# GpSimd's gather loops in two edge stages: the copy of the next indices ahead of the wait for landed gathers, and two rounds in one turn of the loop

## The reference

```python
# third layer (convolution): y = node features after a small matmul
x0e, x1e = y0[edge_src], y1[edge_src]                  # gather by source
m = products of w(edge_scalars), x0e/x1e and edge_sh    # message of an edge
sums = segment_sum(m, edge_dst)                         # sum by destination
# fourth layer (attention)
k = (node_feats @ wk)[senders]; v = (node_feats @ wv)[senders]   # gather by source
alpha = (q[receivers] * w_ij * k).sum(-1) / 4 * cutoffs
out = segment_sum(alpha[..., None] * v, receivers) / 16
```

## Time and profile before

| | us | share of the span |
|---|---|---|
| profiled execution, device time | 9110.68 | |
| its span | 9108.8 | |
| TensorE busy | 7570.4 | 83% |
| VectorE busy | 6053.3 | 66% |
| ScalarE busy | 5236.3 | 57% |
| GpSimd busy | 3425.6 | 38% |
| convolution stage, first to last gather | 3550.8 to 6092.7 | 28% |
| attention stage, first to last gather | 6198.7 to 9056.2 | 31% |

### The profile page before, as it was taken

One profiled execution on the slowest core, in us unless ns is written; L12 is line 12 of the kernel. 1 busy time (PEld: TensorE's weight loads), 2 busy tenths in 40 slices (PEclk: granted clock), 3 DMA queues, 4 the chain that ended last, 5 costly groups with the idle time before them and its releaser, 6 DMA issues. The chain is left out here.

```text
span 9108.8 us, 195691 instructions
## 1 busy us (share of the span) xinstructions
PE 7570.4 (83%) x51013; PEld 5736.6 (63%) x51014; DVE 6053.3 (66%) x12579; ACT 5236.3 (57%) x9302; POOL 3425.6 (38%) x4082
## 2 busy tenths in 40 slices
PE   5999999888869998989998877887777777777775
PEld 3655666577769996666666555555565556555654
DVE  7888998899964446555555555556566656666656
ACT  3666666688757775444444433345556656666653
POOL 0000000000000002666666666655555556566655
PEclk8999999999989998999999888778889888898886
DMA  3333333466646661222222211114555555555554
GB/s 113 138 135 135 137 138 136 153 225 225 213 141 183 183 183 60 63 63 63 63 63 63 55 45 45 45 43 151 159 161 166 161 156 165 166 162 162 165 160 128
DMA packets 511184, 1177.41 MB, mean 129 GB/s; under 512 B 98171, under 2 KB 171308, under 8 KB 491685
## 3 DMA queue, kind: packets, MB, share of 16 engines
q1 hardware_dynamic: 381834, 858.67, 28.9%
q0 software_dynamic: 129280, 317.93, 12.5%
HBM read 899.64 MB, written 276.57 MB: 129 GB/s over the span
## 5 line engine op out<-in xcount | busy, mean ns | idle before, releaser
L2271 POOL DMA_INDIRECT att_kv_rows<-kv_dram,att_stage x1616 | 1632.7, 1010 | 629.7 <-issue 439.2
L2011 POOL DMA_INDIRECT conv_rows<-y_dram,conv_stage x1616 | 1563.3, 967 | 642.2 <-issue 557.3
L695 PE MATMUL conv_part<-conv_msgs,conv_hot 128*128 128x256 f32 x3232 | 939.7, 443 | 0.0
L842 PE MATMUL att_mlp<-mlp_feats,mlp_w 64*128 64x512 f32 x1568 | 522.5, 742 | 435.6 <-ACT mlp_hid L862 429.0
L2034 PEld LDWEIGHTS conv_w_ps<-conv_w,conv_hid 100*128 100x128 f32 x3248 | 466.0, 221 | 656.8 <-issue 314.2
L1967 ACT ACTIVATE conv_hid<-conv_hid_ps 100x512 f32<-100x512 f32 x408 | 243.5, 597 | 1093.7 <-PE conv_hid_ps L2029 701.5
L2086 DVE TENSOR_TENSOR conv_t<-conv_rows,conv_harm 128x384 f32<-128x384 f32 x404 | 226.1, 560 | 953.8 <-DMA conv_rows<-y_dram,conv_stage 947.2
L2034 PE MATMUL conv_w_ps<-conv_w,conv_hid 100*128 100x128 f32 x3248 | 553.6, 322 | 308.1 <-DVE conv_msgs L2100 228.1
L851 PE MATMUL att_mlp<-mlp_w,mlp_hid 128*128 128x128 f32 x6272 | 790.8, 288 | 19.2 <-issue 18.8
L851 PEld LDWEIGHTS att_mlp<-mlp_w,mlp_hid 128*128 128x128 f32 x6272 | 773.1, 204 | 35.7 <-issue 35.2
L695 PEld LDWEIGHTS conv_part<-conv_msgs,conv_hot 128*128 128x128 f32 x3232 | 701.4, 228 | 105.2
(11 more groups left out here) (278 smaller groups left out, 15928.7 us busy)
## 6 DMA issues: line engine op xcount, KB each, us to landing
c_dram<-count_counts SPq DMA_DIRECT2D x392, 392.0 KB, 2.4
mean_counts<-c_dram SPq DMA_DIRECT2D x343, 448.0 KB, 3.4
w_dram<-mlp_w SPq DMA_DIRECT2D x404, 256.0 KB
att_w_rows<-w_dram SPq DMA_DIRECT2D x404, 256.0 KB
soft_counts<-c_dram SPq DMA_DIRECT2D x98, 1024.0 KB, 4.9
mlp_feats<-in_feats SPq DMA_DIRECT2D x405, 192.0 KB
soft_counts<-c_dram SPq DMA_DIRECT2D x49, 1088.0 KB, 5.0
att_lanes<-lo_dram SPq DMA_DIRECT2D x404, 128.0 KB
```

What stands on the lines that cost most here:

```text
L695: ins = nc.tensor.matmul(part, c.hot[:, s, t, :], rows[:, t, :], start=half == 0 and t == 0, stop=half == 1 and t == T - 1)
L842: nc.tensor.matmul(self.hid_ps[:, n], self.w0[rows, m * P:(m + 1) * P], self.feats[rows, :], start=True, stop=True).then_inc(self.hid_sum, 1)
L2011: pool.indirect_dma_start(rows[:, s, t, :], None, y_dram, bass.IndirectOffsetOnAxis(ap=stage[:, s, t:t + 1], axis=0)).then_inc((gathered[s ...
L2271: pool.indirect_dma_start(kv_rows[:, s, t, :], None, kv_dram, bass.IndirectOffsetOnAxis(ap=stage[:, s, t:t + 1], axis=0)).then_inc((gather ...
```

## The change

In both blocks steps 3 and 4 (waits, `turn`, four indirect DMAs) now stand first in a round, then steps 1 and 2 (the wait for round g-2 and the copy of the indices for round g+2), then step 5. What is waited for, and by how much, is the same. The loop over turns becomes one of 49 turns with two old turns in each, and turn 99 is written out beside turn 100.

```diff
 def body(i, first, last=False):
     for s in range(S):
         g = S * i + s
+        pool.wait_ge(staged, g + 1)
+        pool.wait_ge(rows_used, S * i + s + 1)
+        pool.sem_inc(turn, 1)
+        for t in range(T):
+            pool.indirect_dma_start(
+                rows[:, s, t, :], None, y_dram,
+                bass.IndirectOffsetOnAxis(ap=stage[:, s, t:t + 1], axis=0)).then_inc((gathered[s] if t < T - 1 else gathered_last[s]), 16)
         if s < 2 or not last:
             if s >= 2:
                 pool.wait_ge(gathered[s - 2], 16 * (T - 1) * (i + 1))
...
             take((s + 2) % S, g + 2)

-        pool.wait_ge(staged, g + 1)
-        pool.wait_ge(rows_used, S * i + s + 1)
-        pool.sem_inc(turn, 1)
-        for t in range(T):
-            pool.indirect_dma_start(
-                rows[:, s, t, :], None, y_dram,
-                bass.IndirectOffsetOnAxis(ap=stage[:, s, t:t + 1], axis=0)).then_inc((gathered[s] if t < T - 1 else gathered_last[s]), 16)
-
         pool.wait_ge(gathered[s], 16 * (T - 1) * (i + 1))

 take(0, 0)
 take(1, 1)
 body(0, True)
-with pool.Fori(1, NI - 1) as i:
-    body(i, False)
+with pool.Fori(0, NI // 2 - 1) as n:
+    body(2 * n + 1, False)
+    body(2 * n + 2, False)
+body(NI - 2, False)
 body(NI - 1, False, True)
```

More of the change, by code:

```diff
@@ L2257, in body @@
                         g = S * i + s
+                        pool.wait_ge(staged, g + 1)
+                        pool.wait_ge(msg_done, S * i + s + 1)
+                        pool.sem_inc(turn, 1)
+                        for t in range(T):
+                            pool.indirect_dma_start(
+                                kv_rows[:, s, t, :], None, kv_dram,
+                                bass.IndirectOffsetOnAxis(ap=stage[:, s, t:t + 1], axis=0)).then_inc((gathered[s] if t < T - 1 else gathered_last[s]), 16)
                         if s < 2 or not last:
@@ L2265, in body @@
                             take((s + 2) % S, g + 2)
[L2267 to L2273, removed]
                         pool.wait_ge(gathered[s], 16 * (T - 1) * (i + 1))
```

## The result

The changed kernel ran at 9036.2 us (median, 9026.2 to 9058.8), the kernel before beside it at 9110.7 us: a ratio of 0.992 with a 95% interval from 0.990 to 0.994, a gain of 74 us where 144 were forecast.

The account below looks back on a forecast made before the run. GpSimd's gather rounds were taken to bound the kernel, with everybody waiting for GpSimd. Gains of 104 and 72 us less 32 us lost made 144 us, from 9110.7 to 8966.7 us, forecast as 8967 with its own range 8910 to 9030.

Parts of the forecast that it names:

- What bounds the kernel before: Both stages: GpSimd's gather rounds, 6.29 us in the convolution and 7.07 in the attention, set the pace, not TensorE.
- Part A: Three junctions inside an old turn, both stages: register instructions leave the stretch behind the wait; 0.52 us a turn, 104 us.
- Part B: End of an old turn, both stages: loop and count instructions partly go; mean gain 0.36 us a turn, 72 us.
- Part C: Before the gathers: three semaphores waited for in a row cost 0.04 us a round, 32 us lost; ends 0 and 81.
- The double turns: Turn's end, both stages: gain 0.50 us where the new body runs straight on, 0.22 where a branch stays.
- rival 1: Attention: slot-0 landing waits take back what the other slots win; only 72 us gained, 9039 us; chance 0.10.
- "TensorE's 5.73 us in the first part is still under that": Convolution's first part: TensorE's work a round stays below the new 6.11 us round, so it would not become the limit.
- Rival 2: Convolution's first part: TensorE, 91% busy, takes over; the gain of 61 turns, 44 us, is lost; 9011 us; chance 0.08.
- Rival 3: GpSimd's junctions: arithmetic stays behind the landing wait, or landings come later; time as before, 9111 us; chance 0.07.
- Rival 4: GpSimd's junctions: the whole 0.77 us of copy and restart goes each round; 622 us gained, 8489 us; chance 0.03.
- Rival 5: GpSimd's doubled loop body must be fetched each pass; 1.63 us a stall, two a new turn give 9287 us; chance 0.04.

Follow-up runs that it names:

- e6: Kernel before with three of four matmuls a tile left out of the convolution's second perceptron layer; 9116.3 us against 9108.8 for the kernel before.
- e3: New order in both stages with the old one-turn loop, against the kernel before; 8916.0 us, ratio 0.978; again 8917.4 us, ratio 0.979.
- g1: The changed kernel, unaltered, in another session beside the order-only kernel; 8940.7 us against 9120.0 for the kernel before, ratio 0.981.
- g2: New order only, with the old one-turn loop, beside the unaltered changed kernel; 8907.1 us against 9120.0 for the kernel before, ratio 0.977.
- B: Slow session: changed kernel, new order with double turns in one stage only, and gathers running further ahead; kernel before 9103.4 us, changed kernel 9064.9.
- D: Slow session: kernels with a quarter of a TensorE layer less or more, or 56 idle waits; 9060.0 to 9095.1 us, kernel before 9095.0.
- e1: The change in the convolution only, attention as before, against the kernel before; 9050.8 us, ratio 0.993; again 9049.7 us, ratio 0.993.
- session C: Quick session: repeats of order only and convolution only, and both changed kernel and kernel before with less TensorE work; kernel before 9108.8 us.
- e7: Changed kernel, each round waiting for the first three gathers of the round before, not its own; 9727.2 us against 9103.4 for the kernel before.
- e5: Changed kernel with three of four matmuls a tile left out of the convolution's second perceptron layer; 8908.8 us against 9108.8 for the kernel before.

## Why the prediction was right or wrong

**What bounds the kernel before: right.** e6 shows that TensorE's perceptron work doesn't, and e3 shows that GpSimd's junctions do.

**Parts A, B and C: right in mechanism, and nearly in size.** GpSimd's timeline of g1, convolution loop, at the places of the earlier trace rows:

```profile
4501.00 0.94 POOL L2002 DMA_INDIRECT conv_rows<-y_dram,conv_stage  x1 [0.30 <-issue]
4501.94 0.20 POOL L1993 COPY conv_stage<-sources 128x4 int32 x1
4503.06 0.97 POOL L2002 DMA_INDIRECT conv_rows<-y_dram,conv_stage  x1 [0.92 <-DMA conv_rows<-y_dram,conv_stage]
```

The junction is 0.20 + 0.92 = 1.12 us where it was 1.24, and the copy stands at the fourth gather's end (not 0.3 us behind it), released by nothing. The medians of g1 are 1.12, 1.12 and 1.12 us, then 1.20 in the middle of the new body and 1.47 at its end, against my 1.10 to 1.15, 1.22 and 1.50. GpSimd's branches of the loop are halved:

```profile
L2019 POOLq COMPARE_BRANCH  x49: 40/45/53, 3625.6 to 5964.5; - x49
```

Part C's 0.04 us a wait isn't in those junctions: the medians before, less part A's prices, are 1.12, 1.11 and 1.13 us, so it cost nothing that can be seen, and the row of the last turn was the right end. In the convolution of g1 the stage is 79.5 us shorter than in the trace of before, where A, B and C gave 72.

**The double turns: mis-sized.** I gave them the difference of 0.50 and 0.22 us in half the turns, 28 us in all. The junctions show just that (1.20 for 1.45 us), but the whole doesn't: g1 is 34 us behind g2. Their profiled executions differ by 14.9 us, all of it in the attention (15.6 us), where the turn's own end came to 1.80 us for 1.66 and the four gathers of a round took 5.09 us for 5.02. On their own, with the old order, they gained 70 us. The branch was worth removing with the old order and wasn't with the new one; why it loses in the attention is open.

**The attention: rival 1 went the other way.** The junction after slot 0, on average, was 3.48 us before and 2.98 in g1: it gave 0.50 us, not the 0.10 left for it after part C. The gathers' own time grew by 0.08 us a round. The stage lost 99.6 us against 72 priced, so the wait for landings isn't a backlog that takes its share back. That is a mean. The junction of g1 below is longer, at 0.38 + 2.87 = 3.25 us, than the 2.29 + 0.18 + 0.60 of the earlier trace rows; what it shows is that the copy stands ahead of the wait now:

```profile
7518.74 0.38 POOL L2254 COPY att_stage<-sources 128x4 int32 x1
7521.99 1.16 POOL L2263 DMA_INDIRECT att_kv_rows<-kv_dram,att_stage  x1 [2.87 <-DMA att_kv_rows<-kv_dram,att_stage]
```

**"TensorE's 5.73 us in the first part is still under that": the step that failed.** It compares TensorE's busy time with the round, a mean with a mean, and from that puts VectorE's waits for TensorE at nothing. What counts is when TensorE's signal reaches VectorE. In the result VectorE waited for it before 157 of the first part's 240 rounds, for 442 us, most often with the product's matmuls over for more than 1 us by the records, and that held GpSimd's gathers for 114.8 us. In the quick sessions it just suffices: g1 has 126 such waits of VectorE with 270 us, but 21.5 us for GpSimd (13.7 to 30.9 in all of them without altered work), and the 144 us forecast came out as 179. In the result and in B and D it doesn't: GpSimd's waits are 114.8 to 149.2 us in the kernels with the plain wait and without altered work, and the convolution's first part is slower than before the change. Rival 2 was this case as to who waits for whom, at a chance of 0.08 and a price of 44 us, but it named TensorE's being full as the cause. Between g1 and the result the convolution differs by 82 us, of which 62 are the first part's (240 rounds of 0.26 us). Some 19 are the second part's (156 rounds of 0.12 us), where TensorE has a fifth of the time free; between 5180 and 5980 us VectorE waited there for 114.9 us by "remote" in the result and 4.4 in g1. Neither the step nor rival 2 speaks of that part. Rival 2's ceiling was wrong too: I let it take back the gain and not more, but a late signal costs a junction of 3.3 us where it would have been 1.1.

Where the 144 us went, then, from the traces: + 35 us that g1 shows above the forecast, - 82 us in the convolution and - 11 us in the attention by which the result is behind g1; 144 + 35 - 82 - 11 = 86, against 84.4 us between the two profiled spans. That adds up by its making, since g1 and the result are one kernel; what it tells is the place.

**What stays open.** Why TensorE's signals come so late, and why more so in some sessions. That the step above failed is shown; its cause isn't, and the runs that altered TensorE's amount of work moved the round by 0.08 to 0.11 us only. The kernel before doesn't show the pace (9095, 9103 and 9111 us beside the slow ones, 9109 to 9120 beside the quick ones); that GpSimd leaves TensorE room there is my reading. Also, e1's attention has the old kernel's instructions and took 28 us more than e6's in the same session C (2886.9 and 2859.0), which is why a convolution shorter by 81 us made the whole only 59 us faster. No run explains it.

**Rivals 3, 4 and 5** fell: the idle time left the copies, the junctions kept 1.12 us, and no new stall once a turn appeared. The stall that rival 5 took its price from is something else: it stands before every hundredth gather, 16 times in 1616, with 1.9 us of idle time in nearly every one of them, in the kernel before and in the changed one alike. The Trainium skill ("Advanced Engine Details and Errata", ISA Cache) has two cache lines of 256 instructions each. The double body, which I put at some 80 instructions, ran without such stalls, which agrees.

## What to carry to other kernels

Part of what an engine's restart costs behind a wait is register work queued behind that wait, here 0.13 to 0.31 us of 1.26 to 1.76. Put the index arithmetic and small copies ahead of it, look for the same junction in a written-out turn of the trace to price it, and don't count on a saved branch as well: it is paid out of the same stretch. Before saying that an engine at 91% is "still under" the new round, ask when its signals reach the engines that wait for them, and what happens when the slack shrinks (here from 0.56 to 0.38 us a round). Where the answer hangs on that, time both kernels side by side in more than one session, and never compare two versions across sessions: here that first made double turns, then 56 idle waits, look guilty of 100 us and more.

## What the runs showed of the hardware

One and the same kernel took 8940.7 us in one session and 9064.9 in another, both on chip 13 by the record, with the kernel before at 9120.0 and 9103.4 beside it.

An engine that waits for TensorE can start long after the records of the matmuls that it waits for have ended: 6.7 us in the example above, 0.14 us where it goes fastest, and 3.35 us in the median of the result's 157 waits.

GpSimd's indirect gathers have 0.30 us of idle time between two of a round, and mostly 1.9 us before every hundredth. Each stage of every kernel here has 16 such stalls, but for e7's convolution, which has 12.

TensorE can pause inside one group of matmuls that wait for nothing, in steps of some 0.72 us. In the changed kernel's timeline eight matmuls of one group start like this:

```profile
4525.22 0.72 PE L2035 MATMUL conv_w_ps<-conv_w,conv_hid 100*128 100x128 f32 x3
4527.09 0.40 PE L2035 MATMUL conv_w_ps<-conv_w,conv_hid 100*128 100x128 f32 x2 [1.16 <-issue]
4527.82 0.37 PE L2035 MATMUL conv_w_ps<-conv_w,conv_hid 100*128 100x128 f32 x1 [0.33 <-issue]
4528.54 0.78 PE L2035 MATMUL conv_w_ps<-conv_w,conv_hid 100*128 100x128 f32 x2 [0.35 <-issue]
```

4527.09, 4527.82 and 4528.54 are 0.73 and 0.72 us apart. I count such pauses as 0.65 to 1.5 us from one weight load of a group to the next. Between 3640 and 5080 us there is none with the old order in the convolution, 20 to 41 with the new one at the quick pace (3 in e5), 35 to 66 at the slow one and in the result, and 106 in e7. In the attention, between 6350 and 8700 us, there are 0 or 1 with the old order, 7 to 28 with the new one at the quick pace, 39 to 67 at the slow one, and 439 in e7. They go with the slow pace, but they don't make all of it: between 5150 and 5980 us, where the pace differs too, there is at most one outside e7.
